# Row maxima of attention: one transpose per head and a DMA in place of ten transposes, with the rough tiles at other places

## What is computed

```python
def _attention(x, Wqkv, Wproj):
    B, T, D = x.shape
    qkv = (x @ Wqkv).reshape(B, T, 3, H, HD)
    q, k, v = (qkv[:, :, 0], qkv[:, :, 1], qkv[:, :, 2])
    scores = jnp.einsum('bqhd,bkhd->bhqk', q, k) * jnp.float32(HD) ** (-0.5)
    attn = jax.nn.softmax(scores, axis=-1)
    out = jnp.einsum('bhqk,bkhd->bqhd', attn, v).reshape(B, T, D)
    return out @ Wproj
```

## Time and profile before

| | us |
|---|---|
| median of 3 runs | 1533.46 |
| lowest and highest | 1529.39, 1536.1 |
| span of the profiled execution | 1528.7 |
| PE busy in it | 1412.6 (92%) |
| DVE busy | 1154.8 (76%) |
| ACT busy | 970.2 (63%) |
| POOL busy | 493.7 (32%) |

### The profile page before, as it was taken

One profiled execution on the slowest core, in us unless ns is written; L12 is line 12 of the kernel. 1 busy time (PEld: TensorE's weight loads), 2 busy tenths in 40 slices (PEclk: granted clock), 3 DMA queues, 4 the chain that ended last, 5 costly groups with the idle time before them and its releaser, 6 DMA issues.

```text
span 1528.7 us, 25668 instructions
## 1 busy us (share of the span) xinstructions
PE 1412.6 (92%) x8981; PEld 1337.2 (87%) x8981; DVE 1154.8 (76%) x1756; ACT 970.2 (63%) x1658; POOL 493.7 (32%) x366
## 2 busy tenths in 40 slices
PE   3898799999799999999999999999999998699996
PEld 1897577999699999899898998999988898599996
DVE  6788979735689762486877868778788787888885
ACT  7997787522368431366848767478587522599995
POOL 2000000000000010244625536256356501288886
PEclk9999799999899999999999999999999998799999
DMA  7001000122214540000000000000001496476752
GB/s 202 1 1 36 6 14 18 52 100 73 102 54 131 182 142 22 1 21 1 1 21 0 21 0 0 21 0 0 21 1 32 121 296 165 126 155 162 164 94 36
DMA packets 52312, 99.09 MB, mean 65 GB/s; under 512 B 10848, under 2 KB 26852, under 8 KB 52224
## 3 DMA queue, kind: packets, MB, share of 16 engines
q1 hardware_dynamic: 40848, 75.68, 15.9%
q0 software_dynamic: 11376, 22.29, 7.5%
HBM read 67.15 MB, written 44.31 MB: 73 GB/s over the span
## 4 chain that ended last, share of the span: by engine, by line
PE 68%; DVE 9%; issue 3%; DMA 1%; ACT 1%; POOL 1%; POOLq 0%; ACTq 0%; DVEq 0%; SPq 0%
PE ps L372 14%; PE ps L373 14%; PE ps L374 14%; PE ps L823 4%; PE ps L864 4%; PE ps L843 3%; PE ps L866 3%; PE ps L845 3%; PE ps L865 3%; DVE mcol L1072 2%; PE ps L1257 1%; PE ps L598 1%; DVE prlo L1035 1%; PE ps L832 1%; PE ps L1674 1%
## 5 line engine op out<-in xcount | busy, mean ns | idle before, releaser
L1035 POOL TENSOR_TENSOR prlo<-prob,prhi 125x500 fp32r<-125x500 f32 x180 | 251.8, 1404 | 267.9 <-ACT prob L976 266.9
L1072 DVE TENSOR_REDUCE mcol<-ps 125x1 f32<-125x1250 f32 x120 | 174.9, 1458 | 73.0 <-PE ps L823 72.5
L974 ACT ACTIVATE prhi<-ps 125x500 fp32r<-125x500 f32 x300 | 176.8, 589 | 71.4 <-PE ps L845 65.4
L864 PE MATMUL ps<-prhi,vhi 125*128 125x250 f32 x600 | 172.5, 287 | 8.0 <-POOL prlo L1035 3.8
L976 ACT ACTIVATE prob<-ps 125x500 f32<-125x500 f32 x300 | 176.4, 588 | 0.6 <-DVE prlo L1035 0.6
L1529 POOL MEMSET q<- 128x2500 f32 x1 | 2.2, 2187 | 528.4 <-PE ps L374 528.4
L866 PE MATMUL ps<-prlo,vhi 125*128 125x250 f32 x600 | 168.8, 281 | 0.0
L865 PE MATMUL ps<-prhi,vlo 125*64 125x250 f32 x600 | 167.8, 280 | 0.0
L1674 PE MATMUL ps<-ohs,ohd 128*125 128x417 bf16 x380 | 126.0, 384 | 39.9 <-DVE ohs L2110 37.1
L843 PE MATMUL ps<-qst,kst 128*125 128x250 f32 x600 | 156.3, 284 | 3.5 <-ACT q L957 1.4
L372 PE MATMUL ps<-hhi,pthi 125*125 125x384 f32 x400 | 153.7, 384 | 3.0 <-DVE ptlo L712 3.0
(11 more groups left out here) (330 smaller groups left out, 4026.9 us busy)
## 6 DMA issues: line engine op xcount, KB each, us to landing
w1all<-in_L_ffn_W_dram SPq DMA_DIRECT2D x8, 1152.0 KB, 8.4
w2st<-in_L_ffn_W_dram SPq DMA_DIRECT2D x8, 1152.0 KB, 6.4
wqst<-in_L_ffn_Wqkv_dram SPq DMA_DIRECT2D x12, 384.0 KB, 4.2
hid_d<-tin SPq DMA_DIRECT2D x10, 375.0 KB
hin<-hid_d SPq DMA_DIRECT2D x10, 375.0 KB
vtin<-xn_d SPq DMA_DIRECT2D x10, 375.0 KB
out_dram<-accr POOLq DMA_DIRECT2D x10, 375.0 KB, 8.4
xall<-in_x_dram SPq DMA_DIRECT2D x5, 672.0 KB
```

What stands on the lines that cost most here:

```text
L864: pe.matmul(ps[:, b:b + GQ], vhi[:, e, kt, :], hi, start=kt == 0, stop=False)
L974: act.activation(prhi[:, n % RING, :], bank(3 + n % 3, P, 2 * GQ), ACT.Exp, scale=float(HD) ** -0.5)
L1035: eng.tensor_tensor(prlo[:, n % RING, :], prob[:, n % 3, :], prhi[:, n % RING, :].bitcast(f32), ALU.subtract)\
L1072: dve.tensor_reduce(mcol[:, e, t:t + 1], ps[0:P, 0:N], AX.X, ALU.max, negate=True).then_inc(sem("max"), 1)
```

## The change

For each head, one transpose turns the whole `mcol` (125 x 10) into ten rows of 125 (ten partitions of bank 0). ACT copies these 10 x 125 values into a new small buffer `mrow` by one instruction. SP then starts a DMA from `mrow` into the one-partition row of `q2`, and `start` waits for its landing (`m_in`). `m_set` now counts once per head, and tells SP that `mrow` is written; before it writes `mrow` again, ACT waits for the DMA of the head before.

Transpose and copy stand behind unit 21 in both heads. For that the rough tiles end at unit 20: 17 and 18 now follow each other in a head e = 0, and 8 and 9, 11 and 12, 14 and 15, 17 and 18 in a head e = 1.

In SP's list, `m_row` stands behind `load_qk` in each turn of the loop, so that `load_qk` of the turn after comes behind both of them; in pair 5 it stands behind the fourth of the six weight loads. `row2_in` becomes `lnrow_in`, and `gate` moves in memory.

```diff
-        ROUGH_AT = ((3, 5, 7, 9, 11, 13, 15, 17, 19, 21), (6, 8, 10, 12, 14, 16, 17, 19, 21, 22))
+        ROUGH_AT = ((3, 5, 7, 9, 11, 13, 15, 17, 18, 20), (6, 8, 9, 11, 12, 14, 15, 17, 18, 20))
-        MAXIMA_AT = (23, 23)
-        SET_M_AT = (23, 23)
+        MAXIMA_AT = (21, 21)
+        SET_M_AT = (21, 21)
...
             def maxima(p, e):
 
                 pe.wait_ge(sem("max"), 20 * p + 10 * e + T)
-                for t in range(T):
-                    at = (t // 4) * BANK + t % 4 * P
-                    last = pe.transpose(ps[0:1, at:at + P], mcol[:, e, t:t + 1], ident[0:P, 0:P])
-                last.then_inc(sem("m_raw"), 1)
+                pe.transpose(ps[0:T, 0:P], mcol[:, e, :], ident[0:P, 0:P]).then_inc(sem("m_raw"), 1)
...
             def start(p, e, between=lambda j: None):
 
-                pe.wait_ge(sem("m_set"), 4 * p + (2 * e + 2))
+                pe.wait_ge(sem("m_in"), 16 * (2 * p + e + 1))
...
             def set_m(p, e):
-                r = 64 * (1 - e)
                 act.wait_ge(sem("m_raw"), 2 * p + e + 1)
-                act.activation(halves(q2[r:r + 1, e, 0:1000]), two(0, 1, 500), ACT.Copy).then_inc(sem("m_set"), 1)
-                act.activation(q2[r:r + 1, e, 1000:N], bank(2, 1, 250), ACT.Copy).then_inc(sem("m_set"), 1)
+                if e == 1 or not isinstance(p, int) or p > 0:
+                    act.wait_ge(sem("m_in"), 16 * (2 * p + e))
+                act.activation(mrow[:, :], bank(0, T, P), ACT.Copy).then_inc(sem("m_set"), 1)
...
+            def m_row(p, e):
+                r = 64 * (1 - e)
+                sp.wait_ge(sem("m_set"), 2 * p + e + 1)
+                sp.dma_start(q2[r:r + 1, e, :].bitcast(f32).rearrange("o (t c) -> o t c", t=T), mrow[:, :].bitcast(f32)).then_inc(sem("m_in"), 16)
+
             load_qk(0)
             for t in range(8, T):
                 v_in(t)
+            m_row(0, 0)
             with sp.Fori(0, H // 2 - 1) as p:
                 load_qk(p + 1)
+                m_row(p, 1)
+                m_row(p + 1, 0)
...
             sp.wait_ge(sem("qk_raw"), 6 * (H // 2))
-            load_split_sp(sp, 3, wproj, wpst)
+            load_split_sp(sp, 3, wproj, wpst, range(4))
+            m_row(H // 2 - 1, 1)
+            load_split_sp(sp, 3, wproj, wpst, range(4, KD))
```

More of the change, by code:

```diff
@@ L141, in build @@
     zsum = put("zsum", [P, 2, 8], f32)
+    MROW = top[0]
     wsum = put("wsum", [P, T], f32)
     lnc = put("lnc", [P, T, 6], f32)
+    gate = put("gate", [P, T, NE], f32)
+    mrow = put("mrow", [T, P], f32r, at=MROW)
+    assert put.end <= top[0]
     mcol = put("mcol", [P, 2, T], f32)
     viol = put("viol", [128, 4], f32)
-    gate = put("gate", [P, T, NE], f32)
     FREE = top[0]
@@ L374, in three, with load_split_sp @@
             return pe.matmul(o, lhi, rlo, start=False, stop=stop)
-        def load_split_sp(sp, n, dram, stage):
-            for k in range(KD):
+        def load_split_sp(sp, n, dram, stage, chunks):
+            for k in chunks:
                 if k >= 2:
@@ L796, in project @@
                 if not isinstance(p, int):
-                    pe.wait_ge(sem("m_set"), 4 * p)
+                    pe.wait_ge(sem("m_set"), 2 * p)
                 for m in range(2):
@@ L818, in rough @@
                     if e == 1:
-                        pe.wait_ge(sem("m_set"), 4 * p + 2)
+                        pe.wait_ge(sem("m_set"), 2 * p + 1)
                 else:
@@ L1436, in _ @@
             sp.wait_ge(sem("w_lo"), 4 * KD - 1)
-            sp.dma_start(row2[:, 0, :], bcast(ln2g)).then_inc(sem("row2_in"), 16)
+            sp.dma_start(row2[:, 0, :], bcast(ln2g)).then_inc(sem("lnrow_in"), 16)
             sp.wait_ge(sem("w_lo"), 4 * KD)
-            sp.dma_start(row2[:, 1, :], bcast(ln2b)).then_inc(sem("row2_in"), 16)
+            sp.dma_start(row2[:, 1, :], bcast(ln2b)).then_inc(sem("lnrow_in"), 16)
             leave(sp, "sync")
@@ L2327, in _ @@
             dve.tensor_tensor(wrhl[:, :, NE:2 * NE], wrst[:, :, :], wrhl[:, :, 0:NE].bitcast(f32), ALU.subtract).then_inc(sem("route_dve"), 1)
-            dve.wait_ge(sem("row2_in"), 32)
+            dve.wait_ge(sem("lnrow_in"), 64)
             for t in range(T):
```

## The result

The changed kernel takes 1556.8 us (median of four runs, 1554.9 to 1563.8) where the kernel before took 1532.8 beside it: a ratio of 1.016, with a 95% interval of 1.014 to 1.018. It is slower by 24 us. The profiled execution has a span of 1555.7 instead of 1528.7.

A forecast was written before the change was run, and what follows sets the result against it. PE was taken as the bound. Closer tiles less saved transposes, +3.2, the first head's row, +1.1, and pair 5's, +0.1, gave +4.4 us: span 1533.1, median 1538, range 1532 to 1545.

The forecast's parts named there:

- I count both at nothing: Head e = 1 into next: removing the 0.51 `set_m` wait and most of the 0.51 POOL wait gains nothing.
- nothing swallows the cost of closer tiles: In both kinds of head, the net +3.2 us from closer tiles and fewer transposes counts in full.
- POOL beside DVE: At the head's start, POOL starting earlier slows DVE's splitting by up to 0.3 per pair, 1.5 us.
- rival D: PE's clock falls to its lower level in each of five turns: 5 x 3 + 4.4 = +19, 1553; chance 0.06.
- Its trigger: Rival D decides once PE's waits near a head's start reach those ahead of the first head.
- +0.6 as forecast: Per pair of heads, closer tiles less saved transposes: +0.38 in e = 1 and +0.25 in e = 0, 0.63.
- Transposes: Ten transposes become one: 0.96 less on PE per head at 11 of 12 places, 10.6 us.
- Closer tiles: Head e = 1: two more neighbours, 1.34; head e = 0: one neighbour and a transpose wait, 1.21.
- The row: The DMA takes 2.8 (bounds 0 and 4.2), landing 3.6 after the transpose's start; PE needs it at 3.5.
- +1.1: Ahead of the first head, the exposed row delays the first exponential to 641.2: +1.1 us, 0 to 2.5.
- Pair 5: At the end of its head e = 0, the exposed row costs +0.1, up to 1.5 more with a slow DMA.
- the sign of a moved cover: A pair's period below 97.7, against 98.3 forecast, would show neighbours under 0.67 or a moved cover over DVE.

The follow-up runs named there:

- pool_later: Changed kernel with POOL's copy of the next head's values two steps later in each head e = 0: 1555.4 us, ratio 1.014 to before.
- filler: Changed kernel with 22 useless products added in PE's waits at the start of each head e = 0: 1553.7 us, ratio 1.014 to before.
- dma_only: Changed kernel with rough tiles and transposes at their old places, keeping one transpose, copy and DMA: 1527.2 us against 1534.1 before, ratio 0.994.
- e0_new: Changed kernel with the new places in heads e = 0 alone, old ones in heads e = 1: 1536.0 us, ratio 1.000 to before.
- dma_only_again: dma_only, unchanged, measured once more: 1528.4 us against 1537.0 before, ratio 0.994.
- close_t23: Changed kernel with close tiles in heads e = 1 only, both transposes behind unit 23, heads e = 0 as before: 1539.2 us, ratio 1.004.

## Why the prediction was wrong, point by point

- **The step that failed** is "I count both at nothing: PE then only reaches the second weighted step some 1.3 to 1.6 earlier and waits there for DVE, whose list starts and ends when it did." The list did not start when it did: it starts 1.4 later behind unit 24's scores, takes 1.4 longer, and the second weighted step comes 11.3 behind those scores instead of 8.5. The list hangs on unit 24's scores only as long as DVE's work on unit 23 is done by then, and that was so because 2.70 lay between the two units. The two starts stand in the earlier trace rows, and DVE's subtraction in the same view; I priced the pause for PE alone, the wait of 0.54 and the transposes, and not for the engines that used it. The neighbouring sentence, that nothing swallows the cost of closer tiles because "the chain over DVE starts only with unit 24's scores", rests on the same slip.
- **POOL beside DVE.** The mechanism was on record, at no more than 0.3 per pair; splitting grew by 1.4. I had seen one slow piece of four, and since the earlier start of POOL was counted as a small shift I did not ask which other pieces it would reach. The last piece, line 1067, was slow already (2.41 where pool_later has 1.46), and two more became so.
- **The clock** was rival D, at 0.06. Its time, 1553, is near the 1556.8 measured by luck: it has five drops of 3 and no later list, where a drop is worth 1.9 and the later list 2.7 per turn. Its trigger was not met as written either, since the clock fell behind the wait for the rough tile and before the second weighted step. My argument against it was weak. The waits of pair 5 that left the clock at 1.00 were 1.0 and 1.25; here the first is 1.56, and the clock has fallen before the second begins. But no rule follows from such lengths: in pool_later the same two waits, 1.16 and 1.61, stand in each turn, and the clock is low for 3.4 us in one, not at all in one, and for 6.9 in two. Pair 5 showed one surrounding in which such waits do no harm, and I took it for all.
- **The sum of a turn**, then: +0.6 as forecast, +2.7 for the second weighted step, which the late and longer list holds back, and +1.9 for the clock, in all +5.2 of the +5.3 measured. The two new terms are measured apart. The 2.7 is read from the starts in the trace, and filler, which has the list and not the drop, takes 3.35 more per turn than before, close to 0.6 and 2.7. The two halves of the 2.7, late start and longer list, are read from the timeline; no run has the one without the other and all else alike, but the turn of pool_later at a clock of 1.00 shows 0.8 or 0.9 of it to be POOL's copy.
- **Transposes**: right. Ten to one saves 0.96, and dma_only's turn is 1.4 shorter, twice 0.96 less the longer wait at the end of the head e = 1.
- **Closer tiles**: right. 1.21 forecast for a head e = 0 and 1.2 measured; 1.34 forecast for a head e = 1 up to its transpose and 1.4 measured. In the first pair the new places of the head e = 0 seem to cost 3.2 (e0_new against dma_only), but there e0_new has the clock low for 6.9 us and dma_only for 3.4. Against dma_only_again, which has 6.9 too, it is 1.4.
- **The row**: 2.8 taken, 2.0 measured, so it lands 2.7 behind the transpose and not 3.6. In the kernel after PE waits for it once in the loop, 0.31 at 737.85, 3.6 behind its issue; why it was late that once is open. At the first head PE starts at 639.39 instead of 638.86 and the first exponential at 640.14 instead of 640.08, so +1.1 was too much; the first pair as a whole came out at +1.4 against +1.7 forecast, which is within what two executions of one kernel differ by. SP's order cost nothing that these traces show.
- **Pair 5**: +0.1 forecast for its head e = 0 beyond the places, +4.9 measured with them. It has the same start behind the same kind of head as the turns of the loop, with waits of 1.64 and 2.16 that end at 1155.8 and 1159.3. I had looked at its end only.
- **What was to be seen in the profile after** was partly seen: twelve transposes of 0.27, the six waits of 0.33 to 0.42 for `mcol` before rough tiles and those before both transposes of a pair, a wait over 1 us before the second weighted step with DVE as its releaser (0.99 in the fourth turn). The period, forecast at 98.3, is 103.0. I had named a period *below* 97.7 as the sign of a moved cover, and had not looked for one moved the other way.

## What to carry to other kernels

A pause of the engine that bounds a kernel is often the time in which another one finishes; before it is counted as won, follow each engine's list through it and ask what the first instruction of every later chain was queued behind. Then ask it again for the third engine, which now works beside the second. When two edits come together, try each one alone: here the half that did the work was worth 0.6%, and the half that was to make room for it cost nearly four times as much.

## What the runs showed of the hardware

- Where a copy or a subtraction of DVE and an instruction of POOL work at once, both in SBUF, the one that starts second is slowed, and the one that starts first is not. DVE's copy of 64 x 1250 took 1.86 when it began 0.06 behind a POOL subtraction (after), 0.81 when it began 0.05 ahead of one (close_t23) or 0.09 ahead (dma_only), and then POOL's took 1.88 and 1.84 instead of 1.27. DVE's subtraction of the same size takes 1.46 or up to 2.52, one of 125 x 500 takes 0.68 or, in pool_later and close_t23, 1.27. Counted over the attention of all fourteen traces: of 474 DVE subtractions of 125 x 500 beside which POOL began only later, none took over 0.68; of 338 subtractions of POOL beside which a copy or subtraction of DVE began only later, one took over 1.35, and the two had begun within 0.01 of each other. DVE's maximum of 1,250 keys, read from PSUM, is not touched by this: 1.44 to 1.46 in all 1,510 cases, 1,397 of them with POOL at work beside it. Nor is its reciprocal of 128 x 250, in SBUF: 1.70 to 1.72, with POOL or without. So a shift of a tenth of a microsecond can move a microsecond from one engine's list to the other's. The Trainium skill (GPSIMD Engine Reference, 1. Specifications) says that the two share SBUF interfaces and contend when DVE runs in a two-port mode or has two SBUF inputs. The trace agrees.
- The granted clock fell to 0.50 for over 6 us behind a wait of 1.56, in a stretch in which PE was busy for 1.29 of 3 us, and the mean of 0.77 over 15 us is the same in all four turns. Products without a use, put into PE's waits, kept it at 1.00, and the kernel's loop became faster by them. But the length of the waits does not tell by itself: the same two waits in the four turns of pool_later gave means of 0.89, 1.00, 0.77 and 0.77. The Trainium skill (TensorE: Matmul & The Clock Gate, Part 1) has the clock follow how busy the engine has been of late; filler agrees.
- A row of 5 KB, ten partitions to one, lands 2.0 behind its issue on SP wherever PE waits for it in the loop of dma_only and close_t23; in the kernel after it was 3.6 once. The Trainium skill (DMA: Bandwidth & Descriptors, Anatomy of one DMA) gives about 2.0 as the fixed cost on the GpSimd path, which is another one; the 2.0 measured here on SP's is of the same size.
